# Moving the window loads of a graph kernel's two edge stages from SyncE to ScalarE

## What is computed

```python
e_in = jnp.concatenate([x[row], x[col]], axis=-1)
ef = jax.nn.relu(e_in @ ei_w1 + ei_b1) @ ei_w2 + ei_b2
ew = jax.nn.sigmoid(ef @ ew_w + ew_b)[:, 0]
out1 = _layernorm(gelu(_gcn(x, W1, b1, row, col, ew)), ln1_g, ln1_b)
cat = jnp.concatenate([out1[row], out1[col], ef], axis=-1)
ef = _layernorm(ef + (jax.nn.relu(cat @ eu_w1 + eu_b1) @ eu_w2 + eu_b2), lne_g, lne_b)
ew = jax.nn.sigmoid(ef @ ew_w + ew_b)[:, 0]
out2 = _layernorm(gelu(_gcn(out1, W2, b2, row, col, ew)), ln2_g, ln2_b)
```

## Time and profile before

| | us |
|---|---|
| median of 3 runs (lowest, highest) | 8292.19 (8262.65, 8296.35) |
| the profiled execution's own time | 8213.24 |
| span of its profile | 8211.2 |
| first edge stage, from 151 to 2692 | 2541, or 25.2 a step |
| second edge stage, from 3490 to 6343 | 2853, or 28.2 a step |

### The profile page before, as it was taken

The page is one execution under the profiler, slowest core; times in us unless marked ns, Lnnn a source line. Parts: engine busy times, 40 slices in busy tenths (PEclk is TensorE's granted clock), DMA queues, the critical chain, the costliest instruction groups (busy, mean ns, idle before and its releaser), DMA issues. The chain is left out here.

```text
span 8211.2 us, 171843 instructions
## 1 busy us (share of the span) xinstructions
PE 4776.9 (58%) x41016; PEld 3517.8 (43%) x41016; DVE 3950.1 (48%) x17687; ACT 2873.1 (35%) x5414; POOL 3655.2 (45%) x5091
## 2 busy tenths in 40 slices
PE   2111111111111488668888778888888588699997
PEld 1000000000000367545555555555555476578886
DVE  3333323323332688623333333333333688788886
ACT  2222222222222355422222222222223355566664
POOL 3656666666666111155555555555554011411222
PEclk6555555555555667777777787777777667699998
DMA  4554544445555477455555555556555477300000
GB/s 113 141 137 134 139 136 137 136 135 138 139 135 137 137 220 222 143 164 158 160 162 157 156 159 165 161 159 170 160 165 155 132 222 222 106 1 0 0 0 32
DMA packets 1010950, 1117.36 MB, mean 136 GB/s; under 512 B 216893, under 2 KB 749476, under 8 KB 1010441
## 3 DMA queue, kind: packets, MB, share of 16 engines
q1 hardware_dynamic: 852440, 691.61, 28.6%
q0 software_dynamic: 155136, 423.83, 19.4%
q10 hardware_dynamic: 3296, 1.04, 0.1%
HBM read 877.11 MB, written 238.87 MB: 136 GB/s over the span
## 5 line engine op out<-in xcount | busy, mean ns | idle before, releaser
L809 POOL DMA_INDIRECT counts<-tab_pr,idx x1616 | 1550.5, 959 | 1291.5 <-PE pu L1053 594.7
L809 POOL DMA_INDIRECT counts<-tab_p,idx x1616 | 1558.2, 964 | 972.1 <-issue 496.7
L1093 PE MATMUL pz<-tmpb,pieces 96*128 96x64 bf16 x1616 | 149.5, 235 | 1968.6 <-issue 912.9
L907 DVE BATCH_NORM_STATS2 st<-pz 128x6 f32<-128x64 f32 x1616 | 252.7, 219 | 1541.4 <-remote 810.0
L1093 PEld LDWEIGHTS pz<-tmpb,pieces 96*128 96x128 bf16 x1616 | 96.4, 118 | 2049.3 <-issue 2049.3
L1136 ACT ACTIVATE pieces<-pieces,iota_third 96x512 f32<-96x512 f32 x404 | 291.3, 721 | 1818.0 <-DMA tmpb<-tab_q 1063.1
L1053 PE MATMUL pu<-pieces,tmpb 96*128 96x512 f32 x808 | 609.0, 845 | 444.2 <-ACT pieces L1162 330.9
L1063 PE MATMUL pz<-wz,pieces 96*128 96x65 f32 x3232 | 726.1, 311 | 99.3 <-ACT pieces L1165 97.1
L913 DVE TENSOR_TENSOR pieces<-counts,pz 128x256 f32<-128x256 f32 x404 | 169.7, 420 | 1257.0 <-remote 1071.6
L1165 ACT ACTIVATE pieces<-pu,eub 128x512 f32<-128x512 f32 x404 | 277.7, 687 | 1238.5 <-PE pu L1053 797.2
L1064 PE MATMUL pz<-wv,pieces 128*128 128x65 f32 x3232 | 703.1, 303 | 0.0
(11 more groups left out here) (317 smaller groups left out, 9960.5 us busy)
## 6 DMA issues: line engine op xcount, KB each, us to landing
kept_d<-counts SPq DMA_DIRECT2D x808, 256.0 KB
counts<-kept_d SPq DMA_DIRECT2D x808, 256.0 KB
pieces<-rel_d SPq DMA_DIRECT2D x808, 192.0 KB
counts<-srcp_d SPq DMA_DIRECT2D x808, 64.0 KB
counts<-tab_p,idx POOLq DMA_INDIRECT x1616
counts<-tab_pr,idx POOLq DMA_INDIRECT x1616
tmpb<-tab_q SPq DMA_DIRECT2D x808, 12.0 KB
tmpb<-tab_s SPq DMA_DIRECT2D x404, 16.0 KB
```

Source lines behind the costliest of these rows:

```text
L809: pool.indirect_dma_start(out=rows[:, par, u, j, 0:width], out_offset=None, in_=table, in_offset=bass.IndirectOffsetOnAxis(ap=idx[:, 2 * h ...
L907: nc.vector.bn_stats(st16[:, u * SUB + j, :], z[:, j, 0:ED])
```

## The change

In both edge stages the window loads leave SP and go into ACT's list. SP's list keeps only: wait for the gathered rows of a group, store the kept part. In the first stage ACT issues the loads of (it+1, u) right behind its one-hot of (it, u), whose wait for `s_z` guarantees that (it-1, u), which lay in the same buffer, is finished; because its one-hots run two groups ahead of the step, it reads window starts twice a step (for it+1 and it+2). In the second stage ACT issues the loads of (it+2, u) right behind the two relus of (it, u) and reads starts once a step. SP's wait for the used rows goes away.

```diff
                 @block.sync
                 def _(sp):
-                    def windows_of(it, par, k, u, firsts):
-                        i = it * U + u
-                        sp.dma_start(rel_row[:, par, u, :],
-                                     rel_d[ds(i * GE, GE)].rearrange("(o e) -> o e", o=1)
-                                     .broadcast_to([TRI, GE])).then_inc(s_win[par][u], 16)
-                        sp.dma_start(win3[:, par, u, :], tab_q[ds(firsts[u], WIN), :, :].rearrange("w k f -> (w k) f")
-                                     ).then_inc(s_win[par][u], 16)
-                        if update:
-                            sp.dma_start(win[ED:WE, par, u, :], tab_s[ds(firsts[u], WIN), :]).then_inc(s_win[par][u], 16)
...
-                    def step(it, par, k):
-                        firsts = bases_of(SP, it + 1)
+                    def step(it, par, k):
                         for u in range(U):
-                            keep_rows(sp, rows, it - 1, 1 - par, k - 1 + par, u, width)
-                            sp.wait_ge(used, done((it - 1) * U + u))
-                            windows_of(it + 1, 1 - par, k + par, u, firsts)
+                            keep_rows(sp, rows, it, par, k, u, width)
...
                 @block.scalar
+                    def windows_of(it, par, u, firsts):
+                        i = it * U + u
+                        act.dma_start(rel_row[:, par, u, :],
...
-                    def hotT_by_distance(it, par, k, u):
+                    def hotT_by_distance(it, par, k, u, firsts=None):
...
                         nc.scalar.activation(hotT3[:, u, :], apart, ACT.Relu,
                                              bias=1.0, scale=-1.0).then_inc(s_hotT, 1)
+                        if firsts is not None:
+                            windows_of(it + 1, 1 - par, u, firsts)
...
-                    def step(it, par, k, first, last=False):
+                    def step(it, par, k, first, left=3):
+                        if not update and left > 1:
+                            firsts = bases_of(ACTE, it + 1)
+                        if not update and left > 2:
+                            next_firsts = bases_of(ACTE, it + 2)
+                        if update and left > 2:
+                            firsts = bases_of(ACTE, it + 2)
                         for u in range(U):
...
                             if update:
                                 relus(it, u)
+                            if update and left > 2:
+                                windows_of(it + 2, par, u, firsts)
```

More of the change, by code:

```diff
@@ L868, in _ @@
                         sp.dma_start(rows_of(tab_pr)[:, :, 0:ED], big[:, :, 0:ED]).then_inc(s_store, 16)
-                    with sp.Fori(0, (STEPS - 3) // 2) as q:
+                    with sp.Fori(0, STEPS // 2) as q:
+                        step(2 * q, 0, q)
                         step(2 * q + 1, 1, q)
[L871 to L876, removed]
+                    step(STEPS - 1, 0, STEPS // 2)
                     if not update:
@@ L1129, in _, with first_windows @@
                         act.sem_inc(s_, CREDIT)
-                    def hotT_by_distance(it, par, k, u):
+                    def windows_of(it, par, u, firsts):
+                        i = it * U + u
+                        act.dma_start(rel_row[:, par, u, :],
+                                      rel_d[ds(i * GE, GE)].rearrange("(o e) -> o e", o=1)
+                                      .broadcast_to([TRI, GE])).then_inc(s_win[par][u], 16)
+                        act.dma_start(win3[:, par, u, :], tab_q[ds(firsts[u], WIN), :, :].rearrange("w k f -> (w k) f")
+                                      ).then_inc(s_win[par][u], 16)
+                        if update:
+                            act.dma_start(win[ED:WE, par, u, :], tab_s[ds(firsts[u], WIN), :]).then_inc(s_win[par][u], 16)
+                    def first_windows(it, par):
+                        firsts = bases_of(ACTE, it)
+                        for u in range(U):
+                            windows_of(it, par, u, firsts)
+                    def hotT_by_distance(it, par, k, u, firsts=None):
                         i = it * U + u
@@ L1166, in relus @@
                                              bias=eub1[:, 0:1]).then_inc(s_urelu, 1)
-                    def step(it, par, k, first, last=False):
+                    def step(it, par, k, first, left=3):
[5 more added lines that the diff above has]
+                            firsts = bases_of(ACTE, it + 2)
                         for u in range(U):
                             if not update and u + 2 < U:
-                                hotT_by_distance(it, par, k, u + 2)
-                            elif not update and not last:
-                                hotT_by_distance(it + 1, 1 - par, k + par, u + 2 - U)
+                                hotT_by_distance(it, par, k, u + 2, firsts if left > 1 else None)
+                            elif not update and left > 1:
+                                hotT_by_distance(it + 1, 1 - par, k + par, u + 2 - U, next_firsts if left > 2 else None)
                             if update:
                                 relus(it, u)
+                            if update and left > 2:
+                                windows_of(it + 2, par, u, firsts)
                             if update and u == 0 and not first:
@@ L1180, in _ @@
                     act.preload_act_table(ACT.Sigmoid)
-                    if not update:
-                        hotT_by_distance(0, 0, 0, 0)
-                        hotT_by_distance(0, 0, 0, 1)
+                    first_windows(0, 0)
+                    if update:
+                        first_windows(1, 1)
+                    else:
+                        firsts = bases_of(ACTE, 1)
+                        hotT_by_distance(0, 0, 0, 0, firsts)
+                        hotT_by_distance(0, 0, 0, 1, firsts)
                     step(0, 0, 0, True)
@@ L1187, in _ @@
                         step(2 * q + 2, 0, q + 1, False)
[L1188 to L1189 removed]
+                    step(STEPS - 2, 1, STEPS // 2 - 1, False, 2)
+                    step(STEPS - 1, 0, STEPS // 2, False, 1)
                     if update:
```

7 lines of the change are left out of this document (1 added, 6 removed).

## The result

The change came out **1.0% faster**: 8183.5 us median of 4 runs (8174.7 to 8214.8) against 8282.5 us of 4 runs of the kernel before (8262.7 to 8296.4), ratio 0.9897, 95% interval 0.9876 to 0.9917. The forecast was 8440 us, slower. Later comparisons gave the same pair another answer, 1.0025 (1.0016 to 1.0034), and most of what follows is about the difference. The profiled executions stand closer together than the medians: 8190.61 us (span 8188.5) after, 8213.24 (span 8211.2) before, which had been a quick run of its kind. The 23 us between them are, from the first to the last gather of each stage, -42 us in the first edge stage (2498.0 after 2539.8) and +6 in the second (2857.5 after 2851.3), and +13 around them.

A forecast was written before the change was run, and what follows sets the result against it. SP's list was taken to bound the first edge stage, PE with ACT in its chain the second. +80 and +70 us summed to +150, 8440 us on the 8292 us median; own range 8340 to 8600, whole range 7950 to 8750.

The forecast's parts named there:

- SP's list bounds the first stage: First edge stage: SP's issues and reading of window starts fill its 25.2 us step, so SP is late for POOL.
- the stores land a step earlier: First edge stage: SP's four stores cost 2.6 to 14 us, under POOL's 20.3, so they land a step early.
- the kept-row wait loses its cause: First edge stage: POOL's 442 us in 103 waits for the landing of kept rows lose their cause.
- A wait for `used` (L913) is next: First edge stage: POOL's waits for L913 replace those for kept rows, some 500 us or more.
- ACT at 26.0 us a step, +80 us: First edge stage: ACT's added loads and readings make the step 26.0 us, +80 us; bounds 20.8 and 28.5 us a step.
- SP's slow rate: First edge stage, while POOL gathers without pause: 3.6 us a DMA issue and 12 us a reading of window starts.
- readings under 3 us: Sign in the first edge stage: if ACT's readings stay under 3 us, the step carrying ACT's price has failed.
- Second stage +70 us: Second edge stage: ACT's loads and readings, 2.35 us a group, expose 0.17 us a group, 70 us; bounds nothing to 950.
- What holds the others is a long row of gathers: Edge stages: POOL's long unbroken gathers hold other sequencers' DMAs and register loads; SP issued nothing for 15.55 us.
- ACT is not held as SP was: Faster rival, chance 0.30: first stage drops by up to 442 us, second gains 70; 7920 to 8240 us.
- Its price for the case without pauses: Faster rival: first stage drops by up to 442 us, second gains 70, 8292 - 372 = 7920 us.
- No change: Rival, chance 0.11: ACT's and SP's DMA issues take turns at one generator, 25.2 us a step remains, about 8290 us.

The follow-up runs named there:

- 8.2 ms condition: Jobs in which the unchanged kernel before took 8282 or 8225 us; the changed kernel there took 8183.5 us, 0.9897 of it.
- 7.0 ms condition: Jobs in which the unchanged kernel before took 6998 to 7010 us; the changed kernel there took 1.0026 and 1.0025 of it.
- its relatives: SP copies index tiles, ACT loads in one edge stage only, SP in the other; against the kernel before 0.9952 (ACT in second), 0.9946 (ACT in first).

## Why the prediction was wrong, by its steps

1. *SP's list bounds the first stage; the stores land a step earlier; the kept-row wait loses its cause.* The last two were right. The first can hold only in the 8.2 ms condition and there only in part: the order of the stores alone took two thirds of the wait away, and no run tested the length of the list there.
2. *A wait for `used` (L913) is next.* Right, 365 us (forecast: some 500).
3. *ACT at 26.0 us a step, +80 us.* **This term failed**: 24.7 measured, -42 us where +80 was forecast. I had priced ACT's eight issues and two readings at SP's slow rate for the share of the step in which POOL gathers: 3.6 us an issue, 12 a reading. In the profile the second load of a pair followed the first by 1.06 us on the mean (median 0.49; SP before 1.41), and a reading took 2.5 on the mean (a tenth over 6, the longest 13.3; SP before 5.8 by the same reckoning). In all, rows of 0.7 us fill 361 us on ACT, 3.6 us a step, where they filled 633 us, 6.3 a step, on SP. The sign that I had named for this step, readings under 3 us, is there. Where the loads stand goes with it: 287 of ACT's 404 pairs start within 0.3 us of the start of an activation, as in the timeline above, and are 0.53 us apart on the mean; the other 117 are 2.34 us apart. In that timeline the activation had waited for PE's late signal, so the hold was over when ACT issued. That this is why most of them are quick is my reading and not shown: only in 66 of the 287 had ACT been idle for over 2 us before. The forecast carried a price over from one queue to another without its place.
4. *Second stage +70 us.* The mechanism was found, but in another place: 72 us, seen only where POOL's step is shorter than 20.9 us. That the number is nearly the forecast one is luck, for 0.17 us a group was picked between nothing and 2.35 for a stage of 28.2 us a step. In the changed kernel it lay hidden in the 7.0 ms condition behind POOL (2099.4 us against 2097.7 to 2105.0 with SP's loads). In the 8.2 ms condition the stage was 6 us longer; that PE's late signals hid the rest there is likely, and not shown.
5. *What holds the others is a long row of gathers.* In the traces of the 8.2 ms condition, in part: of PE's signals of z that came over 3 us late in the changed kernel, 72% came in a pause of POOL in the first stage (pauses are 20% of its time) and all 101 in the second (32%), there mostly (84%) 2.0 to 3.0 us after the start of the last gather. But POOL also pauses because it waits for PE, so this is an association; and a row of gathers alone holds nothing, as the 7.0 ms condition shows, where POOL breaks its row for little but the copy of indices. What is held was misread too: I named DMAs and register loads, and the rows show register arithmetic and bound checks held for the same 0.7 us each. What makes the condition was not found.
6. *The rivals.* "ACT is not held as SP was" came nearest to the mechanism: ACT was held, but less, and the measured 8183 us lies in that rival's range of 7920 to 8240, near its upper end. Its price for the case without pauses was wrong: I let the first stage fall by up to 442 us, as if nothing stood behind the wait. The waits for L913 did, and PE's late signals with them. "No change" had one stream of issues as its reason. That is not borne out: SP's stores took 0.54 us each on the mean (the longest 0.84) while ACT's loads and readings were held, and the kept rows were no longer late.

The 0.25% loss in the 7.0 ms condition is, as far as the profiles tell, half in the first stage: six traces with ACT's loads there took 2113 to 2123 us from first to last gather (mean 2118), five with SP's 2101 to 2116 (2110). All of the 8 us is in the gathers' own durations (busy 1573 against 1565 us), and the two groups overlap; the other half I could not place. The Trainium skill, DMA: Bandwidth & Descriptors, "Issuing engines are not separate DMA queues", which says that a second issuing engine saves only the time to initiate, agrees with this condition: moving 2020 issues and the readings changed 0.25%. In the 8.2 ms condition the change gave 1.0%, but the stores' order gave 0.5% alone, so what the second issuing engine saved there is open.

**A version that beats both** where POOL bounds is: loads on SP, stores of the step itself, index tile copied by SP: 0.985. In the 8.2 ms condition it was not run; its relatives there gave 0.995.

## What to carry to other kernels

Before a wait is priced as gain, find the next one in line and what it would be worth alone: here 442 us of waits gave 42. ACT's list of issues cost only what it was longer than the bounding engine's step, and a cost that measures as nothing may be covered: shorten the cover (here a copy on POOL) and it appears, 72 us. Before a slow instruction is blamed on what it does, look at its neighbours: here plain register rows took the same 0.7 us as the loads among them. And a trace shows one condition of the machine: time the pair in a second job before believing a per cent.

## What the runs showed of the hardware

- One chip ran one kernel in 7005 and in 8225 us, in two jobs. The difference lies in the stages with indirect gathers. In the slower, PE's semaphore increments come up to 22 us after the recorded end of the matmul in the first stage (ends of matmuls are modelled; ACT, DVE and POOL start only after the increment, so the lateness is real for them). The second load of a pair on SP follows the first by 1.41 us on the mean (median 0.65) instead of 0.53, and a reading of four starts with what follows until the next DMA takes 7.2 us instead of 3.2. The recorded increments of ACT and DVE come within 0.01 us in both.
- In the slower, rows of register arithmetic, bound checks and register loads on SP, DVE and ACT last 0.70 us in long series (1374 such rows in the first stage of the kernel before, at most 14 in a stage of any trace of the other condition), and in the hold that was looked at SP's and DVE's took turns.
- The traces of the slower condition also miss records: of ACT's 401 increments on the one-hot's semaphore in the first stage of the changed kernel 250 are there, in the other condition 395 of 404; of the 25856 increments by which its gathers tell their landing 3083, in the other condition 25524. With so few, when the gathers land can't be compared. One cause that would fit the missing records, the even 0.70 us of whatever row and the lateness is the recording itself. The Trainium skill, NOTIFIC — Programmer's Manual, "When the ring fills", says that a full queue of records either loses new or old ones or holds up the engine that produces them. No run here tests it, and if it is the cause, the 8.2 ms condition would be one of the measurement and not of the kernel.
- A gather on POOL took 0.95 us with 0.30 before the next in both conditions, and 4 to 13% of them, by trace and stage, 1.0 to 1.6 us. Without the copy of indices, some 50 a stage, the first stage was 51 us shorter in the 7.0 ms condition (2050.7 against 2101.4 us, in two jobs), 1.0 us a copy.
- A reading of four window starts takes 1.37 us on SP and 1.38 on ACT when several follow one another (7.0 ms condition).
- A DMA issue of ACT can start 0.15 us after an activation does and run beside it (400 of 404 pairs of loads in the first stage in the 7.0 ms condition stand within 0.3 us of one).
